# Handing over from the features steps of a four-layer vision tower: the wait of all engines is replaced by waits for groups of tiles

## The reference

```python
h = tokens(x)                          # patch embedding, position, class token
h = h + L0_attn(layernorm(h))          # 6 heads, low-rank q, k, v, rotary, causal
h = h + L0_ffn(layernorm(h))           # softmax gate over 32 experts, all of them used
h = h + L1_attn(layernorm(h))          # 12 heads of 64, relative positions
h = h + L1_ffn(layernorm(h))           # 8 experts, the best one for each token
h = h + L2_attn(layernorm(h))          # random features
h = h + L2_ffn(layernorm(h))           # own attention, an MLP, then 4 experts, top 2
h = h + L3_attn(layernorm(h))          # quantised input, base-2 softmax
h = h + L3_ffn(layernorm(h))           # attention with a mixing branch, then an MLP
```

## Time and profile before

| | |
|---|---|
| time, median of 3 runs | 2984.87 us (2984.13 to 2992.16) |
| profiled execution, its own time | 2986.43 us |
| its span | 2984.6 us |
| TensorE busy | 2720.4 us, 91% of the span |
| VectorE busy | 2091.0 us, 70% |
| ScalarE busy | 1060.8 us, 36% |
| mean granted TensorE clock | 0.939 of full |

### The profile page before, as it was taken

How to read it: one execution, slowest core, us unless ns; L and a number is a source line. 1 busy time by engine, 2 the same in 40 slices (tenths; PEclk the granted TensorE clock), 3 DMA queues, 4 the chain that set the end, 5 groups by cost and what they waited for, 6 DMA issues and landing times. The chain is left out here.

```text
span 2984.6 us, 57872 instructions
## 1 busy us (share of the span) xinstructions
PE 2720.4 (91%) x20693; PEld 2468.3 (83%) x20693; DVE 2091.0 (70%) x5299; ACT 1060.8 (36%) x2060; POOL 619.8 (21%) x807
## 2 busy tenths in 40 slices
PE   8889999999999999999999788797988889957778
PEld 7679999999999999999999687676566889945557
DVE  3867777777777776777777788523569567887876
ACT  2433233233333333333333344311555333334433
POOL 1311211211211211211211211021223102022550
PEclk9889999999999999999999899798989889977778
DMA  3011011011011011011001000085000000000000
GB/s 142 17 41 38 20 37 37 19 37 37 19 37 37 19 37 37 19 37 37 19 19 40 2 2 2 22 250 153 1 12 20 38 19 19 1 12 17 25 20 18
DMA packets 24466, 105.65 MB, mean 35 GB/s; under 512 B 4455, under 2 KB 9463, under 8 KB 19086
## 3 DMA queue, kind: packets, MB, share of 16 engines
q1 hardware_dynamic: 22654, 99.62, 9.8%
q0 software_dynamic: 1584, 3.30, 0.3%
HBM read 98.32 MB, written 6.64 MB: 35 GB/s over the span
## 5 line engine op out<-in xcount | busy, mean ns | idle before, releaser
L905 ACT ACTIVATE hid<-bank,dat 128x384 f32<-128x384 f32 (+1 forms) x912 | 554.4, 608 | 1144.0 <-PE bank L595 1031.6
L870 PE MATMUL bank<-w,hid_hi 128*128 128x384 f32 x2964 | 858.5, 361 | 2.2 <-DVE y_tok L921 1.6
L872 PE MATMUL bank<-w,hid_lo 128*128 128x192 f32 x2964 | 745.5, 252 | 0.0
L872 PEld LDWEIGHTS bank<-w,hid_lo 128*128 128x128 f32 x2964 | 570.7, 193 | 1.7
L870 PEld LDWEIGHTS bank<-w,hid_hi 128*128 128x128 f32 x2964 | 561.2, 189 | 5.7 <-issue 4.1
L939 DVE TENSOR_TENSOR hid_lo<-hid,hid_hi 128x384 fp32r<-128x384 f32 (+1 forms) x912 | 539.8, 592 | 31.5
L936 DVE CAST hid_hi<-hid 128x384 fp32r<-128x384 f32 (+1 forms) x912 | 341.0, 374 | 126.2 <-ACT hid L905 124.8
L962 DVE SCALAR_TENSOR_TENSOR h_tok<-bank,gate,h_tok 128x192 f32<-128x192 f32 x416 | 173.6, 417 | 247.0 <-PE bank L872 243.4
L595 PE MATMUL bank<-xa_hi,w_hi 128*128 128x384 f32 (+1 forms) x912 | 324.4, 356 | 8.3 <-DVE w_lo L748 5.1
L595 PE MATMUL bank<-xa_lo,w_hi 128*128 128x384 f32 (+1 forms) x912 | 322.9, 354 | 0.0
L595 PE MATMUL bank<-xb,w_lo 128*128 128x384 f32 (+1 forms) x912 | 322.4, 354 | 0.0
(11 more groups left out here) (359 smaller groups left out, 4296.4 us busy)
## 6 DMA issues: line engine op xcount, KB each, us to landing
raw<-in_L_exp SPq DMA_DIRECT2D x36, 1344.0 KB, 5.7
w_e<-in_L_exp SPq DMA_DIRECT2D x20, 576.0 KB, 3.9
w_e<-in_L_exp SPq DMA_DIRECT2D x20, 384.0 KB
pix<-in_pixels SPq DMA_DIRECT2D x6, 832.0 KB, 10.5
w_e<-in_L_exp SPq DMA_DIRECT2D x20, 195.0 KB
raw<-in_L_mlp SPq DMA_DIRECT2D x2, 1344.0 KB, 5.6
wp_raw<-in_L_att SPq DMA_DIRECT2D x1, 2304.0 KB, 8.3
route_rows<-in_rows_clear SPq DMA_DIRECT2D x1, 2000.0 KB, 22.9
```

What stands on the lines that cost most here:

```text
L870: nc.tensor.matmul(o[:, 0:2 * D], hid_hi[k % 2][:, m, c], w2[j][:, m, :], start=m == 0, stop=False)
L872: ins = nc.tensor.matmul(o[:, 0:D], hid_lo[k % 2][:, m, c], w2[j][:, m, 0:D], start=False, stop=m == HC - 1)
L905: nc.scalar.activation(hid[(6 * k + m) % 3][:, 0:128 * nt], bank[4 + (6 * k + m) % 4][:, 0:128 * nt], func, bias=bias).then_inc(s["h_act"] ...
```

## The change

The diff, cut to its core. In order of the hunks below the banks: the end of `features_phase` (three hunks), the gate logits, the up products of an expert, GpSimd's staging and the projections of attention, and `run`. Left out are the same wait ahead of the second biases and of the mixing branch's logits (there for all 1664 tokens), the variables that carry `lo_full`'s count, and `ahead_of="experts"` at the calls of F2, F7, F8 and F11.

```diff
+        AHEAD_OF = dict(attention=[(0, 0), (6, 7), (4, 5), (2, 3)], experts=[(1, 1), (4, 5), (6, 7), (2, 3)])
+        def x_made(eng, at, cols):
+            group = [128 * (t0 + n) >= cols for t0, n in TBLK].index(True)
+            eng.wait_ge(s["lo_full"].sem, at + group + 1)
...
             def banks(i, n):
-                return bank[2 * i][:, 0:128 * n], bank[2 * i + 1][:, 0:128 * n]
+                first, second = AHEAD_OF[ahead_of][i]
+                y = 128 * n if first == second else 0
+                return bank[first][:, 0:128 * n], bank[second][:, y:y + 128 * n]
...
-                if norm_of is not None:
+                if norm_of is not None and not gate:
                     pe.wait_ge(s["hi_full"].sem, b["hi_full"] + 1)
                     if not plain:
                         pe.wait_ge(s["lo_full"].sem, b["lo_full"] + 1)
-                    keep_clock(bank[0], 4)
+                    keep_clock(bank[AHEAD_OF[ahead_of][0][0]], 2)
...
+            phases[-1]["runs_on"] = not plain
+            x_from["lo_full"] = b["lo_full"]
...
                     for t in range(t0, t0 + nt):
                         c, last = slice(128 * t, 128 * t + 128), t == t0 + nt - 1
+                        x_made(pe, x_at, 128 * (t + 1))
...
+                        if is_first(e):
+                            x_made(pe, x_at, 1280 if k == 0 and m > 1 else 128 * (t0 + nt))
...
                 def stage(t):
+                    x_made(pool, x_at, 104 * t + 104)
...
                 def projections(i, ys):
+                    x_made(pe, x_at, n * i + n)
...
-                eng.wait_ge(s["phase_done"].sem, 3 * (n + 1))
+                if not ph.get("runs_on"):
+                    eng.wait_ge(s["phase_done"].sem, 3 * (n + 1))
```

More of the change, by code:

```diff
@@ L413, in vit_tower, with features_phase @@
         TURNED = [(0, 4), (4, 4), (8, 4), (12, 1)]
-        def features_phase(src, *others, ln=None, norm_of=None, plain=False, keep=None, gate=None, clear=False):
+        AHEAD_OF = dict(attention=[(0, 0), (6, 7), (4, 5), (2, 3)], experts=[(1, 1), (4, 5), (6, 7), (2, 3)])
+        x_from = {}
+        def x_made(eng, at, cols):
+            group = [128 * (t0 + n) >= cols for t0, n in TBLK].index(True)
+            eng.wait_ge(s["lo_full"].sem, at + group + 1)
+        def features_phase(src, *others, ln=None, norm_of=None, plain=False, keep=None, gate=None, clear=False, ahead_of="attention"):
             on_dve = (1, 2)
@@ L784, in experts_phase @@
             STEPS = 24 + TILES
+            x_at = x_from["lo_full"]
             def is_first(e):
@@ L834, in second_biases @@
                         gating["tensor"][2](pe)
+                    x_made(pe, x_at, TOK)
                     for t in range(TILES):
@@ L2307, in vit_tower @@
         attention(l0, h_tok, load)
-        features_phase(n_tok, split, norm_of=h_tok, gate=("L0_g", 32))
+        features_phase(n_tok, split, norm_of=h_tok, gate=("L0_g", 32), ahead_of="experts")
         g = gates(32, "L0_g", "L0_gb", "softmax")
@@ L2324, in vit_tower @@
         attention(l2f, y_tok, load, kept, stats_too=False)
-        features_phase(y_tok, split)
+        features_phase(y_tok, split, ahead_of="experts")
         experts_phase(1, a["L2_mlp"], "L2m_b1", "L2m_b2", y_tok, ACT.Gelu, w, stats_of=y_tok)
@@ L2329, in vit_tower @@
         load, split, w = expert_weights(4, a["L2_exp"], ("w_split", mlp_divided), spread=True)
-        features_phase(n_tok, load, split, ln="ln_L2f2", norm_of=y_tok, gate=("L2_g", 4))
+        features_phase(n_tok, load, split, ln="ln_L2f2", norm_of=y_tok, gate=("L2_g", 4), ahead_of="experts")
         g = gates(4, "L2_g", "L2_gb", "top2")
@@ L2342, in vit_tower @@
         attention(l3f, y_tok, load, kept)
-        features_phase(n_tok, split, ln="ln_L3f2", norm_of=y_tok)
+        features_phase(n_tok, split, ln="ln_L3f2", norm_of=y_tok, ahead_of="experts")
         out_from = made["updated"]
```

1 line of the change is left out of this document (added).

## The result

| | before | after |
|---|---|---|
| time, median of 5 runs | 2984.87 us (2982.83 to 2992.16) | 2965.84 us (2960.85 to 2970.32) |
| ratio, 95% interval | | 0.993 (0.9911 to 0.9949) |
| timed again later, beside other runs of before | 2986.61 us | 2969.28 us, 0.9941 (0.9928 to 0.9955) |
| profiled execution, span | 2984.6 us | 2966.2 us |

The change makes the kernel faster by 21 us by the first ratio and by 18 us by the second. The forecast was 14.1 us, at the edge of the second interval (13 to 22 us) and outside the first (15 to 27 us). The median of 2965.84 us lies at the fast end of the eight-in-ten range (2965 to 2978) and outside the forecast's own range (2967 to 2975).

What follows compares the result with a forecast made beforehand. TensorE, busy for 91% of the span, was taken as the bound, with gains only at phase boundaries. Terms 1.5 + 3.3 + 1.5 + 3.4 + 3.8 + 2.1 - 1.5 = 14.1 us gave 2971 us; eight-in-ten range 2965 to 2978.

Steps and rivals of the forecast that it cites:

- F2: Features phase ahead of the L0 gates: logits start right behind the last transpose, 3.3 us gain, from -0.2 to 4.2.
- F7: Features phase ahead of the L2 MLP: earlier products and first division, up products at higher clock; 3.4 us gain, bounds 1.8 and 4.0.
- F8: Features phase ahead of the L2 gates: logits run with the groups, first gate step earlier; 3.8 us gain, bounds 3.3 and 3.8.
- F1: Features phase ahead of the L0 attention: two fillers less let the projections start earlier, 1.5 us gain.
- F3: Features phase ahead of the L1 attention: weights end the wait, start stays; gain 0, with up to 1.5 us lost.
- F4: Features phase ahead of the routed experts' logits: common wait kept, two fillers less; 1.5 us gain, bounds 0.3 and 2.5.
- F5: Features phase ahead of the L2 attention: longer idle stretch lowers the clock of the head; 1.5 us loss, bounds 0 and 4.0.
- F9: Features phase ahead of the L3 attention: VectorE's `k_x` starts earlier, 2.1 us gain, nothing above it.
- B: Rival across the phase boundaries: the clock takes back half; 6.5 us gain, 2978 us, no change by the bound; 20%.
- C: Rival across the phase boundaries: more than summed, no loss at the L2 attention; 18.1 us gain, 2967 us; 13%.
- D: Rival: starts come earlier, but unseen slack behind them keeps the gain below 3 us, 2983 us; 6%.
- E: Rival at the routed experts: slower, since the clock stays at half there, costing up to 118 us; 4%.

## Why the forecast had the sign right and the size wrong

The columns give what was forecast as gain, by how much the start came earlier (for F5, the end of the head), and by how much the stage became shorter, all in us. Starts are read from the first pair of profiles; stage lengths are means of the two profiles on each side.

| | forecast | start | stage | |
|---|---|---|---|---|
| F1 | 1.5 | 1.4 | 3.5 | start as forecast, and less half clock later |
| F2 | 3.3 | 2.7 | 3.4 | near the forecast |
| F3 | 0 | 0 | 4.3 | the step that failed |
| F4 | 1.5 | 1.5 | 0.3 | the start was eaten by the clock |
| F5 | -1.5 | -2.3 | -2.4 | clock at 0.59 |
| F6 | 0 | | 0.9 | |
| F7 | 3.4 | 1.1 | 2.7 | start forecast too large, clock of the products as forecast |
| F8 | 3.8 | 3.7 | 2.0 | start exact, 2 us given back later |
| F9 | 2.1 | 2.1 | 1.5 | start exact, stage within chance |
| F10, F11 | 0 | | 0.6 | |

The stages sum to 16.8 us; the opening stage takes 1.8 us more on the mean and the mean spans differ by 15.1 us. The timed runs differ by 18 to 21 us, so 3 to 6 us of the gain are in no profile, and no stage can be named for them. That 15.1 is close to the forecast's 14.1 is luck in part, since the terms are off by up to 4.3 us each.

**The step that failed** is "At the four others the clock had already fallen ahead of the first product or at it ... 0, with up to 1.5 lost at F3". Its term at F3 was mis-sized: it priced fewer fillers by the idle stretch in front of the first product alone. The runs put a gain there. The stage is 4.3 us shorter on the means of the two profiles of each side, and 5.2 us shorter with two fillers than with four over thirteen profiles; two fillers less at F3 in the kernel before made the whole kernel 5.4 us (2.7 to 8.4) faster. Undone in the changed kernel, though, F3 cost the whole only 1 us, so the term is sure in the stage and less sure in the sum. With 5 us in place of 0 the sum is 19 us, within both intervals. The errors of the other terms, up to 2 us each, have both signs and sum to -1.6 us. Why the number of fillers acts on this attention stays open.

**F1** had its row right: two fillers less, 1.39 us measured. It missed that the L0 attention would also spend less time at half clock later on (the stage ran at 0.87 before and at 0.88 after, at 0.85 and 0.89 in the second profiles). **F2** rests on group-wise logits, as forecast; its bound from the clock came true in part, as the logits ran at 0.76 in 8.19 us and not at 0.87 in 7.16. The sign named for it, a first logit within 0.5 us of the last transpose, holds for the bias matmul (0.11 us); the first logit proper comes 1.2 us behind the transpose. **F4** fell on its lower bound, 0.3 us: the first logit came 1.46 us earlier in its stage, and the last of them ended at 21.75 in place of 21.79 us, at a clock of 0.61. Here the rival B was right. **F5** lost 2.4 and not 1.5 us, between its bounds. **F7**: the product came 1.86 us earlier in its stage, where 2.6 was forecast, and the twelve ran at 1.00 in 10.65 us, "under 11" as forecast. But the first division was not 1.8 us earlier but 1.1. The forecast took the times of F7's own steps from the trace of before. They came later here, ScalarE's table load by 0.83 us, and the row makes ScalarE the one that held the division. Half clock at the head of the stage lasted longer, and that fits: the first 5.23 us, in which TensorE ran nothing but transposes, are at 0.50, and where the clock had a mean of 0.74 over the 6.45 us up to the end of group 1's low part before, it had 0.64 over the 7.29 us up to the product. The stage's 2.7 us are not the wait's alone either, since with the wait back at F7 and few fillers the stage lost only 0.2 to 0.3 us. At this place row and rule differed. The last transposes (2324.60 to 2326.66 us) and the up products right behind them ran at 1.00. The Trainium skill (TensorE: Matmul & The Clock Gate, Part 4: PE-mode transpose), by which full clock does not engage for transposes, would have had half clock there; the measurement decides against it. **F8** was exact at the start, with VectorE's row free of idle time, as named beforehand, and gave 2 us back where the clock stood at 0.77. **F9** was exact at the start; its stage took 113.6 and 110.9 us in the two profiles of before and 110.8 in both of after, so the gain of the stage is not clear of chance. In four of the five kernels with seven fillers at F5, whose edits do not touch F8 and F9, these stages are 2 to 3 us shorter than in the changed kernel.

**The rivals.** B holds at F4 and in part at F2, not at the up products of F7, and its sum of 6.5 us is out. C, more than summed, has the right total of 18.1 us, but for another reason: it wanted no loss at F5, where 2.4 us were lost, and had nothing at F3. D and E did not happen.

Open stay the chance of the moment in the first 50 us of the L0 experts and in the L1 attention (3 us each between two profiles of one kernel), and why four fillers at F3 are worse than none, two, six or nine. The fastest kernels are the five with seven fillers at F5: 2957.8 to 2962.0 us, ratios 0.9912 to 0.9929, up to 9 us ahead of the changed kernel.

## What to carry to other kernels

A wait and the filler work behind it are one design: remove or keep them together, and measure all four combinations, since here filler removal cost 5 us with the wait and gained 3 to 6 without it, each near the edge of what these intervals can tell. Price a boundary by its start, read from the row of the engine that carries the next stage, and give every start an uncertainty of 2 to 3 us for the half clock that lands elsewhere later. To attribute a difference below 0.5%, profile each kernel at least twice and cut the spans at common waits; one pair of profiles blamed or praised stages by up to 3 us too much.

## What the runs showed of the hardware that was not expected

Busy is not the same as full clock: in the logits behind F4 TensorE ran matmuls of eight columns for 8.26 of 8.26 us and stood at 1.2 GHz throughout, behind transposes, fillers and the first 2.56 us of the same logits at 2.4 GHz. Transposes alone ran at full clock: at F7 for 2.06 us, with nothing but transposes in the 5.23 us ahead of the rise. A change of 2.6 us at one place went with changes of 2 to 3 us in stages 300 to 600 us later, in four of the five kernels that had it, and the new lengths came back within 0.3 us from kernel to kernel. Fillers that end before the weights arrive, and so delay nothing, went with 5 us more in the attention behind them on the mean (four against two; five and eight profiles).
